# Softmax attention in a Macaron block: head pairs through DMA-built operands, or on 64 array rows each

## The chip, the cores and the metric

The kernel runs on one core of one Trainium2 chip. The metric is the device time of one launch in microseconds (us), lower is better. The engines are named as in the profile: PE is TensorE, DVE is VectorE, ACT is ScalarE, POOL is GpSimd, SP is SyncE, whose queue issues DMAs. PEld is the weight load of PE. PSUM is the memory that matmuls write, in banks of 128 x 512 f32.

## What is computed

The program is a chain of stages over x of 8 sequences x 512 tokens x 128 features: a feed-forward stage with block quantisation, softmax attention, the feed-forward stage again, a mixture of experts, six layers of linear attention, the mixture again. Only the softmax attention is touched:

```python
def _L0_attn_ref(x, Wq, Wk, Wv, Wo, bo):     # 16 heads of 64, x is (8, 512, 128)
    q, k, v = (split_heads(x @ W.T) for W in (Wq, Wk, Wv))
    sim = jnp.einsum('bhid,bhjd->bhij', q, k) * 64 ** -0.5
    m = jnp.max(sim, axis=-1, keepdims=True)
    e = jnp.exp(sim - m)
    attn = e / (jnp.sum(e, axis=-1, keepdims=True) + 1e-10)
    out = jnp.einsum('bhij,bhjd->bhid', attn, v)
    return merge_heads(out) @ Wo.T + bo
```

## The kernel before, in words

`attn_stage` works on 64 pairs of heads (8 sequences x 8 pairs), numbered g. It is a software pipeline: one turn of the loop over `PERIODS`, called a period here, does the scores of pair g+1, the exponentials of pair g, the values of pair g-1, the output product of pair g-2 and the projections of pair g+2. The order on each engine is written out by hand in that loop, and semaphores hold the engines together.

Of each pair:

- `project` (L840) makes q, k and v from f16 high and low parts of x and of the weights. `high` (ACT, L748) writes the f16 high part of q or k, `low` (DVE, L681) what is left of it as a second f16.
- `to_rows` (SP, L598) copies these by DMA, so that for each head the high part stands on array rows 0 to 63 and the low part, or the high part again, on rows 64 to 127. Ten DMAs a pair.
- `scores` (L807), eight units i of one head and one tile of 128 queries, is one 128-row matmul of 512 columns each into one of two PSUM banks; `neg_max` (DVE, L664) reads a unit's bank and writes the negated row maxima. After four units `max_turned` (L817) transposes them, `max_row` (DVE, L672) writes four rows of 128 in f16 and `max_row` (SP, L614) brings them by DMA to one row behind the low part.
- `scores_turned` (L824), eight units, is two 128-row matmuls into one of two other banks: all of high times high, high times low, low times high and minus the maximum. `exp` (ACT, L763) reads the bank.
- POOL (L648 to L656) adds up the exponentials of the four key tiles; `values` (PE, L862) sums them over the partitions with ones (L868) and multiplies with v (L875). Both use f32 and half of the array's columns for each head, and each f32 matmul is two instructions on the chip. `total_out` (ACT), `inv_total` (DVE, L689, a reciprocal over 128 x 512) and `normalise` (DVE, L693) follow, then `output` (PE, L879), which adds up in one bank over the eight pairs of a sequence, and `add_x` (DVE, L701).

Two kinds of waiting matter on PE. A unit of scores waits until DVE has read the bank that it overwrites (`s_read`), and `max_turned` until the last read of its head.

Of the kernel before, what the change touches and what calls it, by code (L numbers as in the profile page):

```python
# [543 lines left out]
def attn_stage(nc, mem, tag):  # L544

    with ExitStack() as ctx:
# [12 lines left out]
        nmax = [s.sb(f"nmax{i}", [P, P]) for i in range(2)]  # L561
        mrow = [s.sb(f"mrow{i}", [TPB, P], F16) for i in range(2)]
# [5 lines left out]
        (set_up, proj_done, hi_done, lo_done, v_out, s_done, s_read, t_done, exp_done, chain, added, sums_done, total_done,  # L568
         rinv_done, pv_done, o_done, out_done, biased, x_added) = (s.sem(n) for n in (
             "set_up", "proj_done", "hi_done", "lo_done", "v_out", "s_done", "s_read", "t_done", "exp_done", "chain",  # L570
             "added", "sums_done", "total_done", "rinv_done", "pv_done", "o_done", "out_done", "biased", "x_added"))
        s_in = [s.sem(f"s_in{i}") for i in range(RING)]
        t_in = [s.sem(f"t_in{i}") for i in range(RING)]
        m_in = [s.sem(f"m_in{i}") for i in range(2)]
        S_DMAS, T_DMAS = 8, 2
        halves = (slice(0, DH), slice(DH, P))
        live = lambda g: 0 <= g < PAIRS_ALL
        PERIODS = range(-2, PAIRS_ALL + 2)

        def bank_use(g, j):  # L580

            if g < 0:
                return j if j < 2 else j - 1
            if g == PAIRS_ALL - 1:
                return 9 + 10 * g
            return 9 + 10 * g + j

        UNIT_USE = (0, 1, 3, 4, 6, 7, 8, 9)
        TURN_USE = (5, 2)
        score_use = lambda g, i: bank_use(g - 1, UNIT_USE[i])  # L590
        turn_use = lambda g, head: bank_use(g - 1 + head, TURN_USE[head])

        with nc.Block() as block:

            @block.sync
            def _(sp):
                clear_spent(sp, mem)
                def to_rows(g, which, part_i):  # L598

                    src = part[which]  # L600
                    k = g % RING
                    for head in range(2):
                        rows = src[halves[head], part_i, :]
                        if which == 0 and part_i == 0:
                            sp.dma_start(both[k][0:DH, :, head, :], rows.unsqueeze(1).to_broadcast([DH, 2, SEQ])).then_inc(s_in[k], 16)
                        elif which == 0:
                            sp.dma_start(both[k][DH:P, 0, head, :], rows).then_inc(s_in[k], 16)
                        elif part_i == 0:
                            sp.dma_start(kh[k][0:DH, head, :], rows).then_inc(s_in[k], 16)
                            sp.dma_start(kh[k][DH:P, head, :], rows).then_inc(s_in[k], 16)  # L610
                        else:
                            sp.dma_start(kl[k][0:DH, head, :], rows).then_inc(t_in[k], 16)

                def max_row(g, head):  # L614

                    sp.wait_ge(s_read, turn_use(g, head) + 1)
                    sp.dma_start(both[g % RING][DH:DH + 1, 1, head, :].rearrange("o (t q) -> o t q", q=P), mrow[head][:])\
                      .then_inc(m_in[head], 16)

                sp.wait_ge(set_up, RING + 3)  # L620
                for g in PERIODS:
                    if live(g):
                        max_row(g, 1)
                    if live(g + 2):
                        if g + 2 >= RING:
                            sp.wait_ge(t_done, 8 * (g + 3 - RING))
                        sp.wait_ge(hi_done, 2 * (g + 2) + 1)
                        to_rows(g + 2, 0, 0)
                        sp.wait_ge(lo_done, 2 * (g + 2) + 1)
                        to_rows(g + 2, 0, 1)  # L630
                    if live(g + 1):
                        max_row(g + 1, 0)
                    if live(g + 2):
                        sp.wait_ge(hi_done, 2 * (g + 2) + 2)
                        to_rows(g + 2, 1, 0)
                        sp.wait_ge(lo_done, 2 * (g + 2) + 2)
                        to_rows(g + 2, 1, 1)

            @block.gpsimd
            def _(pool):  # L640
                links = 0
                for g in range(PAIRS_ALL):
                    for head in range(2):
                        if g >= 2:
                            pool.wait_ge(sums_done, g - 1)
# [17 lines left out]
            def _(dve):  # L663
# [54 lines left out]
                for g in PERIODS:  # L718
# [3 lines left out]
                    if live(g):  # L722
                        max_row(g, 1)
# [954 lines left out]
```

## Time and profile before

| | us |
|---|---|
| median of 3 runs | 2222.82 |
| lowest, highest | 2221.43, 2230.84 |
| the profiled execution | 2225.31 |
| its span, first to last instruction | 2223.6 |
| busy in the span: PE | 1599.6 |
| busy: DVE | 1569.2 |
| busy: POOL | 1028.3 |
| busy: ACT | 912.8 |

The rows further down are of two kinds. A row of the timeline begins with the start in us from the span's start and the duration; then come engine, line of the program, operation and what was written from what; "x3" means three instructions merged, and a bracket gives the idle time before and what ended it. The end of a matmul in a row is modelled: it lies some 0.17 us behind the time at which the next can start, so the pace of PE is read from one start to the next.

### The profile page before, as it was taken

To read this page: it belongs to the slowest core of one execution; us is meant where nothing else is said; L and a number is where in the kernel's file an instruction comes from. 1 tells how busy PE (TensorE), PEld (TensorE's weight loads), DVE (VectorE), ACT (ScalarE), POOL (GpSimd) and SP (SyncE) were. 2 spreads that over 40 slices of the span, in tenths; PEclk is the share of its full clock that TensorE was granted. 3 is DMA by queue.
4 is the path that set the end of the run, shared out by engine and by line. 5 is a ranking of instruction groups with operands and counts; after the bars stand their busy time and mean duration, and the time that the engine had idled before them with its cause. 6 is when DMAs were issued, how large, how long until landed. Compare 5 with 4: busy or idle time off the path is not lost. (4 is left out here: it accounts for less than half of the span.)

```text
span 2223.6 us, 29789 instructions
## 1 busy us (share of the span) xinstructions
PE 1599.6 (72%) x9139; PEld 934.4 (42%) x9139; DVE 1569.2 (71%) x3212; ACT 912.8 (41%) x2102; POOL 1028.3 (46%) x1332
## 2 busy tenths in 40 slices
PE   0546389999999999999965563158658888830686
PEld 0334134444444444444423343135437767730453
DVE  5887778878788888877878886336467777752563
ACT  0112255555555555555522221035336676610452
POOL 0111245555555555555532224635435555546353
PEclk9889599999999999999987895579879999955898
DMA  6000022222222222222200000122300000001224
GB/s 186 0 0 1 23 63 58 58 58 58 63 59 61 60 59 58 58 58 59 62 9 1 0 0 24 56 77 80 104 16 1 1 1 1 1 32 62 75 81 145
DMA packets 126010, 104.05 MB, mean 47 GB/s; under 512 B 19680, under 2 KB 120480, under 8 KB 125856
## 3 DMA queue, kind: packets, MB, share of 16 engines
q1 hardware_dynamic: 111616, 77.75, 13.6%
q0 software_dynamic: 8704, 18.89, 2.5%
q10 hardware_dynamic: 5536, 5.52, 0.8%
q8 instruction: 77, 1.26, 0.2%
q14 instruction: 77, 0.63, 0.1%
HBM read 29.32 MB, written 22.30 MB: 23 GB/s over the span
## 5 line engine op out<-in xcount | busy, mean ns | idle before, releaser
L770 ACT ACTIVATE at_pT<-at_turned 128x512 f32<-128x512 f32 x512 | 305.6, 597 | 290.3 <-PE at_turned L837 271.2
L669 DVE TENSOR_REDUCE at_nmax<-at_score 128x1 f32<-128x512 f32 x512 | 337.1, 680 | 69.8 <-PE at_score L814 66.8
L648 POOL TENSOR_TENSOR m_rows<-at_pT 128x512 f32<-128x512 f32 x128 | 162.5, 1269 | 375.1 <-ACT at_pT L770 375.1
L691 DVE RECIPROCAL m_rows<-m_rows 128x512 f32<-128x512 f32 x64 | 214.6, 3353 | 37.7 <-ACT m_rows L776 37.7
L875 PE MATMUL at_pv<-at_pT,at_v 128*64 128x512 f32 x1024 | 230.6, 592 | 0.0
L814 PE MATMUL at_score<-at_kh,at_both 128*128 128x512 f16 x512 | 196.7, 385 | 22.6 <-DVE at_nmax L669 17.0
L1056 POOL DMA_INDIRECT by_token<-m_ysb,m_dest x144 | 138.2, 960 | 144.7 <-DVE m_ysb L1136 109.5
L836 PE MATMUL at_turned<-at_both,at_kh 128*128 128x512 f16 x512 | 194.9, 381 | 0.4 <-ACT at_pT L770 0.3
L837 PE MATMUL at_turned<-at_both,at_kl 128*128 128x512 f16 x512 | 194.8, 380 | 0.0
L656 POOL TENSOR_TENSOR m_rows<-m_rows,at_pT 128x512 f32<-128x512 f32 x128 | 162.8, 1272 | 10.6 <-ACT at_pT L770 0.7
L652 POOL TENSOR_TENSOR m_rows<-m_rows,at_pT 128x512 f32<-128x512 f32 x128 | 162.7, 1271 | 10.4 <-ACT at_pT L770 0.5
L1050 POOL DMA_INDIRECT by_expert<-m_rows,m_slot x128 | 123.7, 966 | 90.7 <-DVE m_slot L1099 53.0
L419 PE MATMUL f_gate<-m_wguT,f_xqT 128*128 128x352 f32 x128 | 63.1, 581 | 104.2 <-DVEq L337 102.9
L1307 PE MATMUL m_h<-m_w,m_x 128*128 x432 | 113.8, 400 | 33.1 <-DVE m_x L1113 23.2
L875 PEld LDWEIGHTS at_pv<-at_pT,at_v 128*64 128x64 f32 x1024 | 73.6, 137 | 146.2 <-issue 146.2
L365 POOL TENSOR_TENSOR f_hq<-f_hg,f_hsc 128x704 f32<-128x704 f32 x32 | 44.4, 1386 | 194.3 <-DVEq L341 194.3
L854 PE MATMUL at_proj<-m_rows 128*128 128x512 f16 x384 | 107.1, 389 | 18.6 <-DVE at_kl L716 10.3
L115 DVE TENSOR_SCALAR la_xn<-la_y,la_ln_mean,la_ln_rstd 128x128 f32<-128x128 f32 x192 | 81.6, 486 | 52.4 <-POOLq L1478 52.4
L381 ACT ACTIVATE f_silu<-f_gate 128x704 f32<-128x704 f32 x32 | 24.2, 757 | 219.7 <-PE f_up L420 219.7
L814 PEld LDWEIGHTS at_score<-at_kh,at_both 128*128 128x128 f16 x512 | 49.5, 97 | 145.5 <-DVE at_nmax L669 61.7
L1296 PE MATMUL m_x<-m_ident,m_xin 128*128 128x128 f32 x144 | 23.0, 284 | 88.6 <-DMA m_xin<-by_expert 88.6
L1124 DVE SCALAR_TENSOR_TENSOR m_g<-m_h,m_xin,m_silu 128x256 f32<-128x256 f32 x144 | 65.3, 478 | 28.1 <-ACT m_silu L1220 14.3
(309 smaller groups left out, 3685.0 us busy)
## 6 DMA issues: line engine op xcount, KB each, us to landing
at_both<-at_part_q SPq DMA_DIRECT2D x128, 128.0 KB, 2.4
at_kh<-at_part_k SPq DMA_DIRECT2D x256, 64.0 KB, 2.0
m_xin<-by_expert SPq DMA_DIRECT2D x144, 72.0 KB
at_both<-at_part_q SPq DMA_DIRECT2D x128, 64.0 KB, 2.1
at_kl<-at_part_k SPq DMA_DIRECT2D x128, 64.0 KB
m_rows<-by_token SPq DMA_DIRECT2D x32, 256.0 KB, 4.8
by_token<-m_ysb,m_dest POOLq DMA_INDIRECT x144
m_x<-in_x SPq DMA_DIRECT2D x8, 256.0 KB, 4.7
```

The lines of the kernel that those rows point to most:

```text
L648: nc.gpsimd.tensor_tensor(acc, pT[g % 2][:, head, 0, :], pT[g % 2][:, head, 1, :], ALU.add).then_inc(chain, 1)
L652: nc.gpsimd.tensor_tensor(acc, acc, pT[g % 2][:, head, 2, :], ALU.add).then_inc(chain, 1)
L656: nc.gpsimd.tensor_tensor(acc, acc, pT[g % 2][:, head, 3, :], ALU.add).then_inc(added, 1)
L669: nc.vector.tensor_reduce(nmax[head][:, qt:qt + 1], score[use % 2][:], AX.X, ALU.max, negate=True)\
L691: nc.vector.reciprocal(rinv, total).then_inc(rinv_done, 1)
L770: nc.scalar.activation(pT[g % 2][:, head, kt, :], turned[i % 2][:], ACT.Exp).then_inc(exp_done, 1)
L814: nc.tensor.matmul(score[use % 2][:], both[k][:, 0, head, qt * P:(qt + 1) * P], kh[k][:, head, :], start=True, stop=True).then_inc(s_done, 1)
L836: nc.tensor.matmul(turned[i % 2][:], kh[k][:, head, tile], both[k][:, 0, head, :], start=True, stop=False)
L837: nc.tensor.matmul(turned[i % 2][:], kl[k][:, head, tile], both[k][:, 1, head, :], start=False, stop=True)\
L875: last = nc.tensor.matmul(pv[halves[head], :], vv[g % 4][:, kt, halves[head]], pT[g % 2][:, head, kt, :], start=(kt == 0), stop=(kt == TPB ...
L1050: nc.gpsimd.indirect_dma_start(dram_rows, bass.IndirectOffsetOnAxis(slot[:, k, t:t + 1], 0), rows[k][:, t, :], None).then_inc(scattered, 16)
L1056: nc.gpsimd.indirect_dma_start(mem["dram_y_all"], bass.IndirectOffsetOnAxis(dest[j // TPB % DESTS][:, j % TPB:j % TPB + 1], 0), ysb[q % YS ...
```

## The change

Each head of a pair now stays on the 64 array rows on which the projection puts it: head 0 on rows 0 to 63, head 1 on rows 64 to 127. The DMAs and their buffers are gone. The scores of a query tile are two 64-row matmuls, one for each head, of the high parts alone, into two banks, `score[0]` and `score[1]`. The turned scores of a key tile are three 64-row matmuls for each head, heads taking turns, then one of four rows for each head that subtracts the maxima: `mdiag` holds 4 x 512 for each head, four maxima rows laid out as a block diagonal, at rows 0 and 32. One transposition of `nmax` serves both heads, and one DVE operation, `max_rows`, multiplies it with the mask `own` into `mdiag`. The maxima are written over the scores' bank (`max_bank`), so the next pair's first scores wait for `m_out`. The program tells the array's shape for each matmul: 128 x 128, 128 rows x 64 columns for sums, values and the transposition, 64 rows x 128 columns for scores and turned scores, 32 x 128 for the maxima.

The order moves as well. On DVE the reciprocal (now `invert`) comes between the reads of query tiles 1 and 2, and `normalise` a period later. On PE the sums and the first values come after the scores of tile 1, the other values are spread over tiles 2 and 3, and v of pair g is projected at the end of period g. POOL alternates the heads. There is one period more at the end.

PE before, the start of a period, from the transposition of head 1's maxima (`at_score<-m_ident,at_nmax`) to the projection of q:

```order
L822 MATMUL at_score<-m_ident,at_nmax 128x128 [waits at_s_read]
L814 MATMUL at_score<-at_kh,at_both 128x512 [waits at_s_read]
L836 MATMUL at_turned<-at_both,at_kh 128x512 [waits at_exp_done]
L837 MATMUL at_turned<-at_both,at_kl 128x512
L854 MATMUL at_proj<-m_rows 128x512 [waits at_v_out]
L854 MATMUL at_proj<-m_rows 128x512 x2
```

PE now, the same engine in the stretch from the third key tile's turned scores to the end of a period:

```order
L755 MATMUL at_turned<-at_high_q,at_high_k 128x512 [waits at_exp_done] x2
L755 MATMUL at_turned<-at_low_q,at_high_k 128x512 x2
L755 MATMUL at_turned<-at_high_q,at_low_k 128x512 x2
L760 MATMUL at_turned<-at_mdiag,at_unit 128x512 x2
L738 MATMUL at_score<-at_high_k,at_high_q 128x512 [waits at_s_read]
L738 MATMUL at_score<-at_high_k,at_high_q 128x512
L804 MATMUL at_pv<-at_pT,at_v 64x512 x2
L743 MATMUL at_score<-m_ident,at_nmax 64x128 [waits at_s_read]
L804 MATMUL at_pv<-at_pT,at_v 64x512 x2
L786 MATMUL at_proj<-m_rows 128x128 [waits at_v_out,at_lo_done]
L786 MATMUL at_proj<-m_rows 128x128 x11
```

Where one unit was three matmuls of 128 rows, a tile is now ten of 64 or four rows, and the transposition stands between two blocks of values.

DVE before, one period, from a pair's reciprocal to the next pair's:

```order
L691 RECIPROCAL m_rows<-m_rows 128x512 [waits at_total_done]
L669 TENSOR_REDUCE at_nmax<-at_score 128x1 [waits at_s_done] x2
L699 TENSOR_TENSOR at_oT<-at_pv,m_rows 128x512 [waits at_out_done,at_rinv_done,at_pv_done]
L669 TENSOR_REDUCE at_nmax<-at_score 128x1 [waits at_s_done] x4
L678 TENSOR_SCALAR at_mrow<-at_score 4x128 [waits at_m_in1,at_s_done]
L669 TENSOR_REDUCE at_nmax<-at_score 128x1 [waits at_s_done] x2
L686 SCALAR_TENSOR_TENSOR at_part_q<-at_proj,at_part_q 128x512 [waits at_hi_done]
L678 TENSOR_SCALAR at_mrow<-at_score 4x128 [waits at_m_in0,at_s_done]
L686 SCALAR_TENSOR_TENSOR at_part_k<-at_proj,at_part_k 128x512 [waits at_hi_done]
```

DVE now, one period in the same way:

```order
L635 RECIPROCAL m_rows<-m_rows 128x512 [waits at_o_done,at_total_done]
L612 TENSOR_REDUCE at_nmax<-at_score 128x1 [waits at_s_done] x2
L628 SCALAR_TENSOR_TENSOR at_low_k<-at_proj,at_high_k 128x512 [waits at_t_done,at_hi_done]
L612 TENSOR_REDUCE at_nmax<-at_score 128x1 [waits at_s_done] x2
L620 TENSOR_TENSOR at_mdiag<-at_score,at_own 64x512 [waits at_t_done,at_m_done]
L612 TENSOR_REDUCE at_nmax<-at_score 128x1 [waits at_s_done,at_m_done]
L612 TENSOR_REDUCE at_nmax<-at_score 128x1 [waits at_s_done]
L642 TENSOR_TENSOR at_oT<-at_pv,m_rows 128x512 [waits at_out_done,at_rinv_done,at_pv_done]
L628 SCALAR_TENSOR_TENSOR at_low_q<-at_proj,at_high_q 128x512 [waits at_t_done,at_hi_done]
L612 TENSOR_REDUCE at_nmax<-at_score 128x1 [waits at_s_done] x2
```

Behind the reciprocal there are now four reads, the low part of k and the maxima before the pair's scores are done; before it was six reads and the normalisation.

The core of the diff; the functions that it takes away are printed above and left out here, and so are ACT's order and the semaphores' names:

```diff
-        both = [s.sb(f"both{i}", [P, 2, 2, SEQ], F16) for i in range(RING)]
-        kh = [s.sb(f"kh{i}", [P, 2, SEQ], F16) for i in range(RING)]
-        kl = [s.sb(f"kl{i}", [P, 2, SEQ], F16) for i in range(RING)]
-        part = [s.sb(f"part_{n}", [P, 2, SEQ], F16) for n in "qk"]
-        vv = [s.sb(f"v{i}", [P, TPB, P]) for i in range(4)]
+        QUAD = P // 4
+        high_of = [[s.sb(f"high_{n}{i}", [P, SEQ], F16) for i in range(RING)] for n in "qk"]
+        low_of = [[s.sb(f"low_{n}{i}", [P, SEQ], F16) for i in range(RING)] for n in "qk"]
+        vv = [s.sb(f"v{i}", [P, TPB, P]) for i in range(2)]
         pT = [s.sb(f"pT{i}", [P, 2, TPB, SEQ]) for i in range(2)]
...
-        nmax = [s.sb(f"nmax{i}", [P, P]) for i in range(2)]
-        mrow = [s.sb(f"mrow{i}", [TPB, P], F16) for i in range(2)]
+        nmax = s.sb("nmax", [P, 2 * QUAD])
+        own = s.sb("own", [2 * QUAD, TPB])
+        mdiag = s.sb("mdiag", [2 * QUAD, TPB, P], F16)
+        unit = s.sb("unit", [2 * QUAD, P], F16)
...
         score = [s.bank(f"score{i}") for i in range(2)]
...
+        max_bank = score[0][0:2 * QUAD, 0:P]
...
                 for g in range(PAIRS_ALL):
...
+                    if g >= 2:
+                        pool.wait_ge(sums_done, g - 1)
+                    for kt in range(1, TPB):
+                        for head in range(2):
+                            acc = psum[g % 2][:, head, :]
+                            before = pT[g % 2][:, head, 0, :] if kt == 1 else acc
+                            pool.wait_ge(exp_done, 8 * g + 2 * kt + head + 1)
+                            if kt > 1:
+                                pool.wait_ge(chain, 4 * g + 2 * (kt - 2) + head + 1)
+                            done = nc.gpsimd.tensor_tensor(acc, before, pT[g % 2][:, head, kt, :], ALU.add)
+                            done.then_inc(chain if kt < TPB - 1 else added, 1)
...
+                def neg_max(g, qt):
+                    if qt == 0 and g:
+                        dve.wait_ge(m_done, g)
+                    for head in range(2):
+                        dve.wait_ge(s_done, 8 * g + 2 * qt + head + 1)
+                        nc.vector.tensor_reduce(nmax[:, head * QUAD + qt:head * QUAD + qt + 1], score[head][:], AX.X, ALU.max, negate=True)\
+                          .then_inc(s_read, 1)
+
+                def max_rows(g):
+                    dve.wait_ge(m_done, g + 1)
                     if g:
...
+                        dve.wait_ge(t_done, 8 * g)
+                    wide = [2 * QUAD, TPB, P]
+                    nc.vector.tensor_tensor(mdiag[:], max_bank.unsqueeze(1).to_broadcast(wide), own[:].unsqueeze(2).to_broadcast(wide),
+                                            ALU.mult).then_inc(m_out, 1)
 
                 def low(g, which):
...
                     dve.wait_ge(hi_done, 2 * g + 1 + which)
+                    if g >= RING:
+                        dve.wait_ge(t_done, 8 * (g - RING + 1))
                     scale = (DH ** -0.5 / W_ATTN, 1.0 / W_ATTN)[which]
...
+                    nc.vector.scalar_tensor_tensor(out=low_of[which][g % RING][:], in0=proj[:], scalar=scale,
+                                                   in1=high_of[which][g % RING][:], op0=ALU.mult, op1=ALU.subtract).then_inc(lo_done, 1)
+
+                def invert(g):
                     dve.wait_ge(total_done, g + 1)
+                    if g:
+                        dve.wait_ge(o_done, g)
                     nc.vector.reciprocal(rinv, total).then_inc(rinv_done, 1)
...
                 for g in PERIODS:
                     if live(g + 1):
                         neg_max(g + 1, 0)
+                    if live(g - 2):
+                        normalise(g - 2)
+                    if live(g + 2):
+                        low(g + 2, 0)
+                    if live(g - 3) and (g - 3) % PAIRS == PAIRS - 1:
+                        add_x((g - 3) // PAIRS)
+                    if live(g + 1):
                         neg_max(g + 1, 1)
-                    if live(g):
-                        max_row(g, 1)
+                    if live(g - 1):
+                        invert(g - 1)
                     if live(g + 1):
                         neg_max(g + 1, 2)
-                        neg_max(g + 1, 3)
-                    if live(g + 2):
-                        low(g + 2, 0)
-                    if live(g + 1):
-                        max_row(g + 1, 0)
                     if live(g + 2):
                         low(g + 2, 1)
-                    if live(g - 1):
-                        inv_total(g - 1)
                     if live(g + 1):
-                        neg_max(g + 1, 4)
-                        neg_max(g + 1, 5)
-                    if live(g - 1):
-                        normalise(g - 1)
-                    if live(g + 1):
-                        neg_max(g + 1, 6)
-                        neg_max(g + 1, 7)
-                    if live(g - 2) and (g - 2) % PAIRS == PAIRS - 1:
-                        add_x((g - 2) // PAIRS)
+                        neg_max(g + 1, 3)
+                        max_rows(g + 1)
...
+                def scores(g, qt):
+                    if qt == 0:
+                        pe.wait_ge(hi_done, 2 * g + 2)
+                    if g or qt:
+                        pe.wait_ge(s_read, 8 * g + 2 * qt)
+                    if g and qt == 0:
+                        pe.wait_ge(m_out, g)
+                    for head in range(2):
+                        rows = halves[head]
+                        nc.tensor.matmul(score[head][:], high_of[0][g % RING][rows, qt * P:(qt + 1) * P], high_of[1][g % RING][rows, :],
+                                         start=True, stop=True).then_inc(s_done, 1)
+
+                def max_turned(g):
+                    pe.wait_ge(s_read, 8 * (g + 1))
+                    nc.tensor.transpose(max_bank, nmax[:], mem["ident"][:]).then_inc(m_done, 1)
+
+                def scores_turned(g, kt):
                     k = g % RING
                     tile = slice(kt * P, (kt + 1) * P)
...
                     if kt == 0:
...
+                        pe.wait_ge(lo_done, 2 * g + 2)
+                    for n, (k_of, q_of) in enumerate(((high_of, high_of), (high_of, low_of), (low_of, high_of))):
+                        for head in range(2):
+                            if n == 0 and (g or kt):
+                                pe.wait_ge(exp_done, 8 * g + 2 * kt + head - 1)
+                            rows = halves[head]
+                            nc.tensor.matmul(turned[head][:], k_of[1][k][rows, tile], q_of[0][k][rows, :], start=(n == 0), stop=False)
+                    if kt == 0:
+                        pe.wait_ge(m_out, g + 1)
+                    for head in range(2):
+                        rows = slice(head * QUAD, head * QUAD + TPB)
+                        nc.tensor.matmul(turned[head][:], unit[rows, :], mdiag[rows, :, :].rearrange("p t q -> p (t q)"), start=False,
+                                         stop=True).then_inc(t_done, 1)
 
...
+                def add_up(g):
                     pe.wait_ge(added, 2 * (g + 1))
                     if g:
                         pe.wait_ge(total_done, g)
                     for head in range(2):
                         last = nc.tensor.matmul(sums[halves[head], :], ones[:], psum[g % 2][:, head, :], start=True, stop=True)
                     last.then_inc(sums_done, 1)
...
+
+                def values(g, kt):
+                    if kt == 0:
+                        pe.wait_ge(v_out, g + 1)
+                        if g:
+                            pe.wait_ge(o_done, g)
+                    for head in range(2):
+                        last = nc.tensor.matmul(pv[halves[head], :], vv[g % 2][:, kt, halves[head]], pT[g % 2][:, head, kt, :],
+                                                start=(kt == 0), stop=(kt == TPB - 1))
+                    if kt == TPB - 1:
+                        last.then_inc(pv_done, 1)
...
-                    for i in range(UPP):
+                    for kt in range(TPB):
+                        if live(g):
+                            scores_turned(g, kt)
                         if live(g + 1):
-                            scores(g + 1, i)
-                        if live(g):
-                            scores_turned(g, i)
-                        if i == 1 and live(g):
-                            max_turned(g, 1)
-                        if i == 2 and live(g + 2):
-                            project(g + 2, 0)
-                        if i == 3:
-                            if live(g - 2):
-                                output(g - 2)
+                            scores(g + 1, kt)
+                        if kt == 0:
+                            if live(g + 2):
+                                project(g + 2, 0)
+                            if live(g - 3):
+                                output(g - 3)
+                        elif kt == 1 and live(g - 1):
+                            add_up(g - 1)
+                            values(g - 1, 0)
+                        elif kt == 2:
                             if live(g + 2):
                                 project(g + 2, 1)
+                            if live(g - 1):
+                                values(g - 1, 1)
+                        elif kt == 3:
+                            if live(g - 1):
+                                values(g - 1, 2)
                             if live(g + 1):
-                                max_turned(g + 1, 0)
+                                max_turned(g + 1)
                             if live(g - 1):
-                                values(g - 1)
-                        if i == 6 and live(g + 2):
-                            project(g + 2, 2)
+                                values(g - 1, 3)
+                            if live(g):
+                                project(g, 2)
```

## Rows read from the trace of the kernel before

**Rows 1.** Busy time of each engine by stretch, the pipeline's steady part.

```profile
core 0: us, PE busy (x) PEld busy (x) DVE busy (x) ACT busy (x) POOL busy (x), PEclk, DMA share, GB/s
290.00:1120.00 830.00, 806.39 (x4409) 358.69 (x4409) 666.30 (x868) 440.39 (x738) 474.91 (x377) 1.00 0.24 60
```

**Rows 2.** Timeline, PE and its weight loads (PEld), one period from 701 us.

```profile
701.13 0.38 PE L836 MATMUL at_turned<-at_both,at_kh 128*128 128x512 f16 x1
701.13 0.10 PEld L837 LDWEIGHTS at_turned<-at_both,at_kl 128*128 128x128 f16 x1
...
701.56 0.81 PE L854 MATMUL at_proj<-m_rows 128*128 128x512 f16 x3
...
702.21 0.38 PE L814 MATMUL at_score<-at_kh,at_both 128*128 128x512 f16 x1
...
702.86 1.05 PE L887 MATMUL at_out<-m_woT,at_oT 128*128 128x128 f32 x8
...
703.97 0.82 PE L854 MATMUL at_proj<-m_rows 128*128 128x512 f16 x3
...
704.63 0.27 PE L822 MATMUL at_score<-m_ident,at_nmax 128*128 128x128 f32 x1
...
704.83 0.20 PEld L868 LDWEIGHTS at_sums<-m_rows 128*64 128x64 f32 x4 [0.28 <-issue]
704.83 1.08 PE L868 MATMUL at_sums<-m_rows 128*64 128x512 f32 x4
...
705.74 3.60 PE L875 MATMUL at_pv<-at_pT,at_v 128*64 128x512 f32 x16
...
709.28 0.39 PE L814 MATMUL at_score<-at_kh,at_both 128*128 128x512 f16 x1
...
711.23 0.83 PE L858 MATMUL at_proj<-m_rows 128*128 128x128 f16 x12
...
711.90 0.38 PE L814 MATMUL at_score<-at_kh,at_both 128*128 128x512 f16 x1
...
713.85 0.27 PE L822 MATMUL at_score<-m_ident,at_nmax 128*128 128x128 f32 x1
...
715.02 0.81 PE L854 MATMUL at_proj<-m_rows 128*128 128x512 f16 x3
```

**Rows 3.** Timeline, ACT and DVE, the same period.

```profile
702.41 0.60 ACT L755 ACTIVATE at_part_q<-at_proj 128x512 f16<-128x512 f32 x1
...
702.63 0.69 DVE L669 TENSOR_REDUCE at_nmax<-at_score 128x1 f32<-128x512 f32 x1 [0.60 <-PE at_score L814]
...
703.24 0.68 DVE L686 SCALAR_TENSOR_TENSOR at_part_q<-at_proj,at_part_q 128x512 f16<-128x512 f32 x1
...
705.96 0.60 ACT L776 ACTIVATE m_rows<-at_sums 128x512 f32<-128x512 f32 x1 [0.53 <-PE at_sums L868]
...
706.59 3.35 DVE L691 RECIPROCAL m_rows<-m_rows 128x512 f32<-128x512 f32 x1 [0.44 <-ACT m_rows L776]
...
709.86 1.22 DVE L669 TENSOR_REDUCE at_nmax<-at_score 128x1 f32<-128x512 f32 x2
...
711.00 0.68 DVE L699 TENSOR_TENSOR at_oT<-at_pv,m_rows 128x512 f32<-128x512 f32 x1
...
711.59 2.71 DVE L669 TENSOR_REDUCE at_nmax<-at_score 128x1 f32<-128x512 f32 x4
...
714.22 0.27 DVE L678 TENSOR_SCALAR at_mrow<-at_score 4x128 f16<-4x128 f32 x1
```

**Rows 4.** Waits, 252 to 1150 us, PE for a DMA: us in total, times, longest.

```profile
PE at_score L814 <- DMA at_kh<-at_part_k: 5.5, 3, 2.5
```

**Rows 5.** Timeline, start of the attention stage.

```profile
252.65 0.17 DVE L708 MEMSET at_nmax<- 128x128 f32 x1 [3.93 <-PEq L483]
...
260.14 1.46 PE L854 MATMUL at_proj<-m_rows 128*128 128x512 f16 x3 [10.25 <-DVE at_kl L716]
```

More of the change, by code:

```diff
@@ L597, in _ @@
                 clear_spent(sp, mem)
[L598 to L612, printed above, removed]
@@ L681, in low @@
                 def low(g, which):
                     dve.wait_ge(hi_done, 2 * g + 1 + which)
+                    if g >= RING:
+                        dve.wait_ge(t_done, 8 * (g - RING + 1))
                     scale = (DH ** -0.5 / W_ATTN, 1.0 / W_ATTN)[which]
-                    pair = part[which]
-                    nc.vector.scalar_tensor_tensor(out=pair[:, 1, :], in0=proj[:], scalar=scale, in1=pair[:, 0, :], op0=ALU.mult,
-                                                   op1=ALU.subtract).then_inc(lo_done, 1)
@@ L785, in _ @@
                     if live(g):
[L786 to L788 removed]
+                        exp(g, 1)
                     if live(g - 1):
@@ L801, in _ @@
                 XY = [(0, 0), (0, 1), (1, 0)]
-                def bank_free(use):
-                    if use >= 2:
-                        pe.wait_ge(s_read, use - 1)
-                def scores(g, i):
-                    head, qt = divmod(i, TPB)
-                    use = score_use(g, i)
-                    k = g % RING
-                    if i == 0:
-                        pe.wait_ge(s_in[k], 16 * S_DMAS * (g // RING + 1))
-                    bank_free(use)
-                    nc.tensor.matmul(score[use % 2][:], both[k][:, 0, head, qt * P:(qt + 1) * P], kh[k][:, head, :], start=True,
-                                     stop=True).then_inc(s_done, 1)
@@ L833, in scores_turned @@
-                    n = 8 * g + i
-                    if n >= 2:
-                        pe.wait_ge(exp_done, n - 1)
-                    nc.tensor.matmul(turned[i % 2][:], kh[k][:, head, tile], both[k][:, 0, head, :], start=True, stop=False)
-                    nc.tensor.matmul(turned[i % 2][:], kl[k][:, head, tile], both[k][:, 1, head, :], start=False, stop=True)\
-                      .then_inc(t_done, 1)
+                        pe.wait_ge(lo_done, 2 * g + 2)
[5 more added lines that the diff above has]
+                            nc.tensor.matmul(turned[head][:], k_of[1][k][rows, tile], q_of[0][k][rows, :], start=(n == 0), stop=False)
@@ L869, in values @@
                     last.then_inc(sums_done, 1)
-                    pe.wait_ge(v_out, g + 1)
-                    if g:
-                        pe.wait_ge(o_done, g)
-                    for kt in range(TPB):
-                        for head in range(2):
-                            last = nc.tensor.matmul(pv[halves[head], :], vv[g % 4][:, kt, halves[head]], pT[g % 2][:, head, kt, :],
-                                                    start=(kt == 0), stop=(kt == TPB - 1))
-                    last.then_inc(pv_done, 1)
+                def values(g, kt):
+                    if kt == 0:
+                        pe.wait_ge(v_out, g + 1)
+                        if g:
+                            pe.wait_ge(o_done, g)
+                    for head in range(2):
+                        last = nc.tensor.matmul(pv[halves[head], :], vv[g % 2][:, kt, halves[head]], pT[g % 2][:, head, kt, :],
+                                                start=(kt == 0), stop=(kt == TPB - 1))
+                    if kt == TPB - 1:
+                        last.then_inc(pv_done, 1)
                 def output(g):
```

160 lines of the change are left out of this document (41 added, 119 removed).

## The prediction

> **What bounds the kernel now.** I read first the busy time by stretch: from 290 to 1120 us PE is busy 806 of 830 us at full clock, DVE 666, POOL 475, ACT 440, and the DMA engines 0.24 of their time [rows 1]. So PE is the bound of the attention stage, and DVE is next. Then the timeline of one period. The projection of q begins at 701.56 and the next one at 715.02 [rows 2]: a period is 13.46 us, and the 830 us hold 62 of them. PE's row durations overlap, so I price by starts [rows 2]. Two f16 matmuls of 512 columns take 701.13 to 701.56, 0.215 each, and three take 0.65 (701.56 to 702.21). Twelve of 128 columns take 0.67 (711.23 to 711.90). Eight f32 instructions of 128 columns last 1.05 with a last one of about 0.27, so 0.11 each and 0.89 in all. Sums and values, twenty f32 instructions of half the columns, take 704.83 to 709.28, 4.45.
>
> The values' sixteen took 3.54 (705.74 to 709.28). One f32 instruction of 512 columns is two f16 slots, 0.43. One after the other sixteen would be 6.9; in pairs they are 3.44. So matmuls on two halves of the columns do run at once here, and about 0.10 is left over at the end, where the array goes back to the full shape. At the entry it is alike: the transposition starts at 704.63, is worth 0.11, and the sums start at 704.83 together with their weight load, which elsewhere comes a matmul ahead (the load of 701.13 runs beside the matmul of 701.13) [rows 2]. I call this a shape change and price it at 0.10.
>
> PE's period before: 24 score slots 5.16, projections 1.30 and 0.67, sums and values 4.35, output 0.89, two transpositions 0.22, two shape changes 0.20: 12.79. The other 0.67 of 13.46 is waiting.
>
> **What the change does to PE.** A tile's scores become two 64-row matmuls, its turned scores six, its maxima two of four rows. If the two heads run at once, as column halves do, that is 1 + 3 + 1 slots a tile, 20 a period or 4.30: 0.86 less. One transposition goes, 0.11 less. The sum is 11.62 without shape changes. But now the shape changes often. Between the 64-row, 32-row, full and half-column shapes I count 18 in a period: four in tile 0, with the one from the period before, four in tile 1, five in tile 2, five in tile 3. At 0.10 they cost 1.80, and PE's work is 13.42, just the old period. No row shows a change between row shapes. From below it could cost nothing, from above I take twice the column price, 0.20. I take 0.10, the one price that rows show.
>
> The Trainium skill (TensorEngine Tiling (Array Packing), Key Properties) says that changing the tiling mode, not just the tile, drains TensorE. The rows show such a stall for columns only; by the page all 18 would pay, which is the value taken.
>
> **What the change does to DVE.** The work is about the same: eight reads, two low parts, reciprocal, normalisation, and one `max_rows` of 512 elements, at most the 0.68 of the normalisation [rows 3], for two of 0.27. Its place is what counts. With data at hand DVE starts a read 0.57 after the one before (two from 709.86 to 711.00), the normalisation's successor 0.59 after it (711.00 to 711.59), and the read behind the reciprocal 3.27 after its start (706.59 to 709.86) [rows 3]. PE goes on 0.73 after the start of the DVE operation that it waits for (703.24 [rows 3] to 703.97 [rows 2]).
>
> Before, the reciprocal lay beside the values' 3.54 on PE, in which no scores were wanted. Now PE does 0.86 of values and then wants scores of tile 2 and 3, whose reads stand behind the reciprocal. This closes a loop from one reciprocal to the next:
>
> - DVE: reciprocal 3.27, two reads 1.14, low part of k 0.59, first read of tile 3 0.57, and from the start of the last read to the transposition on PE 0.73: 6.30.
> - PE, transposition to sums: 0.11, last values 0.86, v 0.67, turned scores and maxima of tile 0 0.86, scores 0.215, q 0.65, output 0.89, turned scores and maxima of tile 1 0.86, scores 0.215: 5.33, and nine shape changes.
> - Sums to reciprocal: 1.13 to `total_out` (704.83 to 705.96) and 0.63 more (706.59) [rows 2, 3].
>
> That is 13.4 with free shape changes and 14.3 with nine at 0.10. PE has 13.42 of work in it, so 0.9 is waiting, which must stand before the scores of tile 3 (they wait for reads behind the reciprocal) and before the transposition (it waits for both reads of tile 3, with only 0.86 of values to do meanwhile). In both the longest single wait is under 1 us, so I leave the clock at full.
>
> **The rest.** The ten DMAs a pair, SP's queue and their buffers go: PE waited for them three times in the whole stage, 5.5 us [rows 4], so in the steady part that is worth nothing. ACT and POOL have the same operations in another order; both had half of the period free [rows 1], and that room hides it. `max_rows` ends about 1.1 after the transposition (713.85 [rows 2] to 714.22 [rows 3], then 0.73), while PE still has 0.86 + 0.67 + 0.65 to do before the maxima are wanted: hidden, with 1 us to spare. At the start 7.5 us of memsets (252.65 to 260.14) shrink to some 2 [rows 5], and the 5.5 of waits for DMAs go: 11 us gained once. The end stays a chain of the same steps: nothing.
>
> **The sum.** 62 x (14.30 - 13.46) = 52, less 11, is 41 us more on the profiled execution's 2225.3 (its span is 2223.6). That execution lies 2.5 above the median of the runs, 2222.8, so I forecast 2264 us.
>
> **The rivals.**
>
> - **A, the forecast**: heads run at once, a shape change costs 0.07 to 0.13. 14.0 to 14.6 a period: 2245 to 2283. Chance 0.50.
> - **B, not slower**: changes between row shapes are free, and only those to and from the half-column shape pay. It is one mechanism, in the loop above: two of its nine changes are of that kind, so the period is 13.6, 9 us more over 62, less 11: 2221. If those are free too, 13.4 gives 2208. It decides below 0.02 a change. For it: column halves take other columns of results, row halves only feed other rows, and no row shows that this needs a stop. Against it: at 704.83 even the weight load waited [rows 2]. Chance 0.20.
> - **C, dearer**: a change costs 0.2, or the loads of the next 64 rows are not hidden (20 slots with a load of 0.10 [rows 2] exposed in each is 2.0 a period, the same size). PE's work is 15.2 then, 15.6 with 0.4 of waiting before the transposition: 62 x 2.14 - 11 = 122, 2345. Chance 0.15.
> - **D, the change doesn't do what it says**: the heads' matmuls don't run at once, 20 slots more, 4.30. PE's work is 17.7: 62 x 4.24 - 11 = 252, 2475; with free shape changes 15.9 and 2363. For it: no row shows two row halves at once. Against: the column halves do it. Chance 0.12.
>
> In this trace the weight load for the next matmul on the same rows runs beside the present one (both at 701.13 [rows 2]). The Trainium skill (TensorE: Matmul & The Clock Gate, What overlaps and what doesn't) says that a load overlaps matmuls in flight only when the row group differs; by that rule each head's next matmul would wait for its load, which is C's second form, and the row speaks against it. The same page gives 3.07 for four row tiles instead of 4; an estimate by that ratio makes the 20 slots 5.6 instead of 4.3, some 80 us more, between A and C. No row here shows it.
>
> **How the numbers follow.** 0.03 is left for what I don't see. About 0.5% is what a measurement of this kernel tells from no change, so the bounds are 2211.7 and 2233.9. Faster: nearly half of B, 0.09. Same: the rest of B and the cheap end of A, 0.16. Slower: 0.75. The range goes from just under B's lower end, 2207, over A and C to the cheap end of D, 2385; most of D is left out.
>
> **What would show it.** In the trace after: two rows of the turned scores that start together, or 0.2 apart (D). The start of the first maxima matmul 0.10 later than 0.65 after the first turned one (A), or not (B). The third scores pair some 0.3 late and the transposition some 0.6 late, both released by `neg_max`, and ACT and POOL idle beside it. A period of 14.3 from one q projection to the next. If PE never waits for `neg_max`, my loop is wrong; if the clock falls below 1.00, all prices are too low.

## The result

| | before | changed |
|---|---|---|
| median, us | 2224.31 | 2276.23 |
| lowest, highest | 2221.43, 2230.84 | 2271.47, 2277.21 |
| span of the profiled execution | 2223.6 | 2275.1 |

The changed kernel is slower: 1.0225 times the time of before, 95% interval 1.0197 to 1.0253. The forecast was 2264, and slower. The DMAs of the attention stage are gone, and so is any wait for them; PE is busy for longer, 1660.7 us of the span against 1599.6.

This is PE's timeline of the changed kernel over the end of one period and all of the next, with one row of its weight loads and with DVE's and ACT's rows that stand in the loop of the prediction. "x2" are the two heads' matmuls.

```profile
700.99 0.82 PE L781 MATMUL at_proj<-m_rows 128*128 128x512 f16 x3
...
701.64 1.05 PE L816 MATMUL at_out<-m_woT,at_oT 128*128 128x128 f32 x8
...
702.63 0.39 PE L755 MATMUL at_turned<-at_high_q,at_high_k 64*128 64x512 f16 x2
702.64 0.10 PEld L755 LDWEIGHTS at_turned<-at_low_q,at_high_k 64*128 64x128 f16 x2
702.86 0.38 PE L755 MATMUL at_turned<-at_low_q,at_high_k 64*128 64x512 f16 x2
...
703.07 0.38 PE L755 MATMUL at_turned<-at_high_q,at_low_k 64*128 64x512 f16 x2
703.38 0.39 PE L760 MATMUL at_turned<-at_mdiag,at_unit 4*128 4x512 f16 x2
703.70 0.39 PE L738 MATMUL at_score<-at_high_k,at_high_q 64*128 64x512 f16 x2
...
704.02 1.08 PE L795 MATMUL at_sums<-m_rows 128*64 128x512 f32 x4
...
705.15 0.60 ACT L706 ACTIVATE m_rows<-at_sums 128x512 f32<-128x512 f32 x1 [0.26 <-PE at_sums L795]
705.78 3.35 DVE L635 RECIPROCAL m_rows<-m_rows 128x512 f32<-128x512 f32 x1 [0.36 <-ACT m_rows L706]
...
709.05 1.22 DVE L612 TENSOR_REDUCE at_nmax<-at_score 128x1 f32<-128x512 f32 x2
...
709.81 0.39 PE L760 MATMUL at_turned<-at_mdiag,at_unit 4*128 4x512 f16 x2
710.19 0.68 DVE L628 SCALAR_TENSOR_TENSOR at_low_k<-at_proj,at_high_k 128x512 f16<-128x512 f32 x1
...
710.33 0.39 PE L738 MATMUL at_score<-at_high_k,at_high_q 64*128 64x512 f16 x2
710.65 1.08 PE L804 MATMUL at_pv<-at_pT,at_v 128*64 128x512 f32 x4
710.78 1.28 DVE L612 TENSOR_REDUCE at_nmax<-at_score 128x1 f32<-128x512 f32 x2
...
712.12 0.30 PE L743 MATMUL at_score<-m_ident,at_nmax 128*64 128x128 f32 x1 [0.40 <-DVE at_nmax L612]
712.35 1.08 PE L804 MATMUL at_pv<-at_pT,at_v 128*64 128x512 f32 x4
...
713.36 0.84 PE L786 MATMUL at_proj<-m_rows 128*128 128x128 f16 x12
714.14 0.39 PE L755 MATMUL at_turned<-at_high_q,at_high_k 64*128 64x512 f16 x2
...
715.21 0.39 PE L738 MATMUL at_score<-at_high_k,at_high_q 64*128 64x512 f16 x2
...
715.53 0.82 PE L781 MATMUL at_proj<-m_rows 128*128 128x512 f16 x3
```

From one q projection to the next is 14.54 us (700.99 to 715.53), against 13.46 before [rows 2]. Three pairs of 64-row matmuls start 0.22 apart (702.63, 702.86, 703.07), so both heads fit in one slot: they run at once. To the four-row pair it is 0.31, and from there to the scores 0.32 (703.38 to 703.70), each a slot of 0.215 and 0.10 for the change of shape. The scores of tile 3 come 0.52 after the maxima of their tile (709.81 to 710.33) where others come 0.32 after: 0.20 of waiting for the reads behind the reciprocal. The transposition comes 1.47 after the values that it follows (710.65 to 712.12), which take 1.01 elsewhere (712.35 to 713.36): 0.46 of waiting.

The stage's start and end, from the first write of its setup to the first turned scores, and its last operation; of the changed kernel:

```profile
251.18 0.11 DVE L650 MEMSET at_nmax<- 128x64 f32 x1 [3.91 <-PEq L483]
...
252.08 1.46 PE L781 MATMUL at_proj<-m_rows 128*128 128x512 f16 x3 [3.64 <-DVE at_own L656]
...
266.94 0.61 PE L755 MATMUL at_turned<-at_high_q,at_high_k 64*128 64x512 f16 x2
```

```profile
1198.43 0.69 DVE L648 TENSOR_TENSOR m_x<-at_out,m_x 128x512 f32<-128x512 f32 x1 [1.25 <-PE at_out L816]
```

and the same last operation of the kernel before:

```profile
1150.64 0.69 DVE L706 TENSOR_TENSOR m_x<-at_out,m_x 128x512 f32<-128x512 f32 x1 [1.25 <-PE at_out L887]
```

The stage took 947.9 us (251.18 to 1199.12) and before 898.7 (252.65 [rows 5] to 1151.33). That is 49.2 of the 51.5 between the spans; the other 2.3 come up in stages that the change doesn't touch (1.5 less ahead of this one, 3.7 more behind it). The 64 reciprocals give the mean period and the start apart. Their first and last starts, of the kernel before and of the changed one:

```profile
L691 DVE RECIPROCAL m_rows<-m_rows x64: 3352/3353/3354, 301.4 to 1145.3; 128x512 f32<-128x512 f32 x64
```

```profile
L635 DVE RECIPROCAL m_rows<-m_rows x64: 3352/3353/3353, 284.6 to 1193.0; 128x512 f32<-128x512 f32 x64
```

Over 63 periods 843.9 became 908.4: 13.40 to 14.42 us each, 64.5 in all. From the stage's start to the first reciprocal 48.8 became 33.4, 15.4 less. Part of that is the clock. In the kernel before, PE waited 2.48 for a DMA, and after it worked at the lower of its two clock levels, 1.2 GHz, until 286 us: the granted clock is 0.51 from 280 to 286, where a slot takes 0.43. In the changed kernel the granted clock is 1.00 from 271 us to the first reciprocal. The wait and the stretch of the kernel before, and the stretch of the changed one (columns as in [rows 1], the granted clock is the third number from the end):

```profile
280.53 0.61 PE L814 MATMUL at_score<-at_kh,at_both 128*128 128x512 f16 x1 [2.48 <-DMA at_kh<-at_part_k]
```

```profile
280.00:286.00 6.00, 5.47 (x14) 2.14 (x15) 2.35 (x4) 1.79 (x3) 1.72 (x2) 0.51 0.10 24
```

```profile
271.00:285.00 14.00, 12.15 (x81) 4.08 (x79) 9.56 (x15) 8.31 (x15) 9.04 (x8) 1.00 0.01 1
```

### The profile page after: what moved, and what is told of

The parts are those of the page before. It is cut to its first block and busy times, and to the rows that moved or that the text cites. A ratio compares the mean times of both kernels' runs of the same rounds, so it can differ in the third digit from the quotient of the medians.

```text
span 2275.1 us, 30856 instructions
## 1 busy us (share of the span) xinstructions
PE 1660.7 (73%) x10099; PEld 874.6 (38%) x10099; DVE 1561.2 (69%) x3141; ACT 880.7 (39%) x2102; POOL 1022.4 (45%) x1332
## 5 line engine op out<-in xcount | busy, mean ns | idle before, releaser
L612 DVE TENSOR_REDUCE at_nmax<-at_score 128x1 f32<-128x512 f32 x512 | 324.9, 676 | 188.2 <-PE at_score L738 188.1
L700 ACT ACTIVATE at_pT<-at_turned 128x512 f32<-128x512 f32 x512 | 277.9, 594 | 301.1 <-PE at_turned L760 301.1
L804 PE MATMUL at_pv<-at_pT,at_v 128*64 128x512 f32 x1024 | 272.0, 611 | 0.0
L692 ACT ACTIVATE at_v<-at_proj 128x512 f32<-128x512 f32 x64 | 38.2, 597 | 185.2 <-PE at_proj L786 185.2
L738 PE MATMUL at_score<-at_high_k,at_high_q 64*128 64x512 f16 x512 | 100.8, 390 | 11.7 <-DVE at_nmax L612 3.0
L755 PE MATMUL at_turned<-at_high_q,at_high_k 64*128 64x512 f16 x512 | 101.5, 388 | 0.5 <-ACT at_pT L700 0.4
L760 PE MATMUL at_turned<-at_mdiag,at_unit 4*128 4x512 f16 x512 | 99.4, 385 | 0.0
L755 PE MATMUL at_turned<-at_low_q,at_high_k 64*128 64x512 f16 x512 | 98.6, 377 | 0.0
L755 PE MATMUL at_turned<-at_high_q,at_low_k 64*128 64x512 f16 x512 | 98.5, 377 | 0.0
L804 PEld LDWEIGHTS at_pv<-at_pT,at_v 128*64 128x64 f32 x1024 | 56.7, 135 | 86.9 <-issue 79.4
```

The lines of the kernel that those rows point to most:

```text
L612: nc.vector.tensor_reduce(nmax[:, head * QUAD + qt:head * QUAD + qt + 1], score[head][:], AX.X, ALU.max, negate=True)\
L700: nc.scalar.activation(pT[g % 2][:, head, kt, :], turned[head][:], ACT.Exp).then_inc(exp_done, 1)
L738: nc.tensor.matmul(score[head][:], high_of[0][g % RING][rows, qt * P:(qt + 1) * P], high_of[1][g % RING][rows, :], start=True, stop=True). ...
L755: nc.tensor.matmul(turned[head][:], k_of[1][k][rows, tile], q_of[0][k][rows, :], start=(n == 0), stop=False)
L760: nc.tensor.matmul(turned[head][:], unit[rows, :], mdiag[rows, :, :].rearrange("p t q -> p (t q)"), start=False, stop=True).then_inc(t_don ...
L804: last = nc.tensor.matmul(pv[halves[head], :], vv[g % 2][:, kt, halves[head]], pT[g % 2][:, head, kt, :], start=(kt == 0), stop=(kt == TPB ...
```

## The experiments

**Theory L**: the period is the loop from one reciprocal to the next, over DVE's reads and PE's queue, with 0.10 for each change of shape. **Rival W**: the period is PE's own work, and the reciprocal's place costs nothing. Periods below run from one start of v's projection to the next, medians between 300 and 1080 us, where they repeat to 0.01; read so, the changed kernel's is 14.54, and that is the one to compare with. (The mean between the first and the last reciprocal would not do: it also moves when the reciprocal is moved.) Times are beside runs of before on the same chip (median 2227.79 for the first four).

**Maxima in the scores' shape** (`e1_max64`).

```diff
-        nmax = s.sb("nmax", [P, 2 * QUAD])
-        own = s.sb("own", [2 * QUAD, TPB])
-        mdiag = s.sb("mdiag", [2 * QUAD, TPB, P], F16)
-        unit = s.sb("unit", [2 * QUAD, P], F16)
+        nmax = s.sb("nmax", [P, P])
+        own = s.sb("own", [P, TPB])
+        mdiag = s.sb("mdiag", [P, TPB, P], F16)
+        unit = s.sb("unit", [P, P], F16)
...
-                        rows = slice(head * QUAD, head * QUAD + TPB)
+                        rows = halves[head]
```

> The changed kernel with the maxima's block diagonal spread over each head's 64 rows (zeros in rows 4 to 63), so that its matmuls have the shape of the scores; the transposition becomes a full 128 x 128. Shape changes on PE fall from 18 to 12 a period, on the loop through the reciprocal from 9 to 6, and the transposition costs 0.11 in place of 0.23. Theory L (the period is the loop from one reciprocal to the next, at 0.10 a shape change): period 14.5 less 0.42, 14.1 us, time 2276 - 26 = 2250. Rival W (the period is PE's own work, the reciprocal's place costs nothing): 0.72 less, 13.8, time 2231. If shape changes were free: 2270 or more.

Measured 2251.59, ratio 1.0106 (1.0077 to 1.0134), period 14.15 for L's 14.1. One tile of its timeline, PE, with the slot of the maxima now like the others:

```profile
707.41 0.39 PE L755 MATMUL at_turned<-at_high_q,at_high_k 64*128 64x512 f16 x2
707.64 0.38 PE L755 MATMUL at_turned<-at_low_q,at_high_k 64*128 64x512 f16 x2
707.85 0.38 PE L755 MATMUL at_turned<-at_high_q,at_low_k 64*128 64x512 f16 x2
708.07 0.38 PE L760 MATMUL at_turned<-at_mdiag,at_unit 64*128 64x512 f16 x2
708.28 0.38 PE L738 MATMUL at_score<-at_high_k,at_high_q 64*128 64x512 f16 x2
...
714.07 0.38 PE L760 MATMUL at_turned<-at_mdiag,at_unit 64*128 64x512 f16 x2
714.90 0.39 PE L738 MATMUL at_score<-at_high_k,at_high_q 64*128 64x512 f16 x2 [0.45 <-DVE at_nmax L612]
```

The maxima follow 0.22 after and the scores 0.21 after them, so the 0.10 goes with the shape, not with the operation. But the scores of tile 3 now wait longer (0.83 from 714.07 to 714.90): PE reaches them sooner and DVE doesn't. Of the 0.72 of work that the expectation counts, 0.39 came out. That is L, not W.

**The reciprocal at the end of the period** (`e2_inv_end`).

```diff
                         neg_max(g + 1, 1)
-                    if live(g - 1):
-                        invert(g - 1)
...
                         max_rows(g + 1)
+                    if live(g - 1):
+                        invert(g - 1)
```

> The changed kernel with one thing moved: the reciprocal stands on DVE behind the pair's maxima, at the end of the period, in place of between the reads of tiles 1 and 2. Theory L: the loop is opened, the scores of tile 3 wait no longer, PE's work with its 18 shape changes and the wait of some 0.4 before the transposition are left: period 14.2, time 2276 - 19 = 2257. Rival W: no change, 2276. If the reads of tile 0 behind the reciprocal now come too late: slower than 2276.

Measured 2260.11, ratio 1.0141 (1.0122 to 1.0160), period 14.32 (708.15 to 722.47 below) for L's 14.2, 0.22 less than the changed kernel's. W's 2276 is excluded: against 1.0225 the interval lies clear. In the steady part PE's matmuls wait for DVE at the transposition alone:

```profile
PE at_score L743 <- DVE at_nmax L612: 21.1, 57, 0.4
```

```profile
708.15 0.84 PE L786 MATMUL at_proj<-m_rows 128*128 128x128 f16 x12
...
722.47 0.84 PE L786 MATMUL at_proj<-m_rows 128*128 128x128 f16 x12
```

**Both** (`e3_both`).

> Both edits, maxima in 64 rows and the reciprocal at the end of the period. Theory L: with the loop opened the six saved shape changes count in full, period 13.4, time 2276 - 70 = 2206, below the kernel before. Rival W: as the first edit alone, 2231. The sum of the two single gains would be 2231 as well by L, so anything near 2206 says that the loop and the shape changes hid one another.

Measured 2214.38, ratio 0.9926 (0.9904 to 0.9949), period 13.51. The single gains are 0.39 and 0.22 us a period, both together 1.03: each edit alone runs into what the other takes away. With the reciprocal at the end the 64-row maxima are worth 0.81, alone 0.39. The time is 8 us above L's figure and 17 below W's; put to the 2224.31 that these figures started from, the ratio gives 2208, 2 above L's. What PE still waits for is the transposition:

```profile
706.55 1.08 PE L804 MATMUL at_pv<-at_pT,at_v 128*64 128x512 f32 x4
...
708.00 0.33 PE L743 MATMUL at_score<-m_ident,at_nmax 128*128 128x128 f32 x1 [0.37 <-DVE at_nmax L612]
...
709.27 0.84 PE L786 MATMUL at_proj<-m_rows 128*128 128x128 f16 x12
```

**The reciprocal in halves, the transposition behind the values** (`e4_split`), with the maxima in 64 rows.

```diff
-                    nc.vector.reciprocal(rinv, total).then_inc(rinv_done, 1)
+                    nc.vector.reciprocal(rinv[:, 0:SEQ // 2], total[:, 0:SEQ // 2])
+
+                def invert_rest(g):
+                    nc.vector.reciprocal(rinv[:, SEQ // 2:], total[:, SEQ // 2:]).then_inc(rinv_done, 1)
...
                         max_rows(g + 1)
+                    if live(g - 1):
+                        invert_rest(g - 1)
...
-                            if live(g + 1):
-                                max_turned(g + 1)
                             if live(g - 1):
                                 values(g - 1, 3)
+                            if live(g + 1):
+                                max_turned(g + 1)
```

> Maxima in 64 rows; the reciprocal in two halves of 256 columns, one in its place of the changed kernel, one at the end of the period; the transposition behind the last values, so that they cover the reads of tile 3. Theory L: no read of scores is late for longer than PE has other work, shape changes 10 a period, period 12.8, time 2276 - 107 = 2169. Rival W: 12.8 of work too if the halves cost nothing, but then the first edit alone would have shown 13.8 or less. If each half costs much more than 1.68 on DVE: 2190 or more.

Measured 2167.20, ratio 0.9726 (0.9706 to 0.9745), period 12.81 for L's 12.8. This version beats both kernels. DVE's timeline shows the two halves, each between reads that are not late:

```profile
701.76 1.74 DVE L638 RECIPROCAL m_rows<-m_rows 128x256 f32<-128x256 f32 x1
703.42 1.22 DVE L612 TENSOR_REDUCE at_nmax<-at_score 128x1 f32<-128x512 f32 x2
...
707.54 1.74 DVE L635 RECIPROCAL m_rows<-m_rows 128x256 f32<-128x256 f32 x1
709.20 1.22 DVE L612 TENSOR_REDUCE at_nmax<-at_score 128x1 f32<-128x512 f32 x2
```

PE's rows around the transposition:

```profile
711.73 1.94 PE L809 MATMUL at_pv<-at_pT,at_v 128*64 128x512 f32 x8
713.60 0.33 PE L748 MATMUL at_score<-m_ident,at_nmax 128*128 128x128 f32 x1
713.76 0.83 PE L791 MATMUL at_proj<-m_rows 128*128 128x128 f16 x12
```

From the start of the last two blocks of values to v's projection it is 2.03 (711.73 to 713.76), and in `e3_both`, with the transposition between the blocks, 2.72 (706.55 to 709.27). These 0.69 are nearly all of the 0.70 between the two periods, so the gain over `e3_both` lies at the transposition, which no longer waits. No run moves the transposition and leaves the reciprocal whole, so what the halves add by themselves is not shown.

**The reciprocal cut short in its place** (`e7_short`).

```diff
-                    nc.vector.reciprocal(rinv, total).then_inc(rinv_done, 1)
+                    nc.vector.reciprocal(rinv[:, 0:64], total[:, 0:64]).then_inc(rinv_done, 1)
```

> The changed kernel with seven eighths of the inversion left out: from the third pair on the reciprocal covers 64 of 512 columns, some 0.5 us in place of 3.35; the rest of rinv keeps old values, so the output is not the reference's. Its place stays. Theory L: the loop through the reciprocal falls below PE's own work, which with the wait before the transposition is 14.2: time 2276 - 19 = 2257, as when the reciprocal was moved, not 3 us a period less. Rival W (PE's own work alone): 2276. Rival DVE (the reciprocal counts in full): 14.5 - 2.8, time 2100.

Measured 2267.11 beside 2232.28 for before, ratio 1.0161 (1.0131 to 1.0192); 1.0161 of 2224.31 is 2260, for L's 2257. Against the expectation's words the edit leaves out seven eighths of every reciprocal, not from the third pair on only:

```profile
L635 DVE RECIPROCAL m_rows<-m_rows x64: 552/553/554, 284.3 to 1178.2; 128x64 f32<-128x64 f32 x64
```

The period is 14.32, 0.22 less for 2.8 us less of DVE work, and the same to 0.01 as in `e2_inv_end`. So the loop through the reciprocal held the period up by what it stood above PE's work with its wait before the transposition, and no more; moving the reciprocal did as much as leaving most of it out. The rival in which it counts in full, 2100, is out.

**Shape changes alone** (`e8_split_max32`): the version in halves with `nmax`, `own`, `mdiag`, `unit` and the maxima's rows as in the changed kernel.

> The fastest version so far (reciprocal in two halves, transposition behind the last values, maxima in 64 rows, 2167) with the maxima in 4 rows of a 32-row shape again, as in the changed kernel. There PE never waited for the reads, so this prices shape changes without a loop in between: 18 a period against 10, and the transposition to half the columns 0.23 against 0.11. At 0.10 a change: 0.92 a period, 2167 + 57 = 2224. If the saved time of the 64-row maxima came from elsewhere (from the loop alone): 2167 to 2180.

Measured 2224.19 beside 2232.28 for before, ratio 0.9964 (0.9952 to 0.9976), period 13.63. Against 12.81 that is 0.81 for eight changes of shape, 0.10 each. In the steady part of neither does the profile show a wait of PE for a read. That the time met 2224 is partly luck: 0.9964 of the 2227.79 beside the first version is 2220. The other 0.12 of the expected 0.92 was for the transposition, and it didn't come. PE's rows around it:

```profile
711.72 1.94 PE L809 MATMUL at_pv<-at_pT,at_v 128*64 128x512 f32 x8
713.59 0.30 PE L748 MATMUL at_score<-m_ident,at_nmax 128*64 128x128 f32 x1
713.73 0.83 PE L791 MATMUL at_proj<-m_rows 128*128 128x128 f16 x12
```

To v's projection it is 2.01 (711.72 to 713.73), where the version in halves, with its transposition in the full shape, takes 2.03. The transposition starts 1.87 after the values in both (713.59, 713.60). Eight value instructions are worth 1.72 and a block behind another shape 0.05 more (the four sums took 0.91 before, 704.83 to 705.74 [rows 2]), so 0.10 is left before the transposition even here, where the shape stays 128 x 64. It is as if the transposition to half the columns stood in a shape of its own; why, no run tells.

**Head by head** (`e5b_by_head`).

```diff
-                    for n, (k_of, q_of) in enumerate(((high_of, high_of), (high_of, low_of), (low_of, high_of))):
-                        for head in range(2):
+                    for head in range(2):
+                        for n, (k_of, q_of) in enumerate(((high_of, high_of), (high_of, low_of), (low_of, high_of))):
```

> The changed kernel with the six 64-row matmuls of a tile's turned scores issued head by head, three for head 0 and then three for head 1, in place of heads taking turns. Same work, same number of shape changes. If two row halves run at once only where neighbours in the queue lie on different halves (theory L's reading of the rows that start together), the six take 5 slots of 0.215 in place of 3: 1.7 us more work on PE a period, and with the rest of the loops some 1.5 more, time 2276 + 93 = 2369. Rival: PE starts what is further back in its queue by itself, then nothing changes, 2276.

Measured 2201.72 beside 2152.01 for before on that chip, ratio 1.0228 (1.0207 to 1.0250): the changed kernel's 1.0225; the period is 14.56, for 14.54. My expectation fell. PE's timeline:

```profile
691.83 0.40 PE L755 MATMUL at_turned<-at_high_q,at_high_k 64*128 64x512 f16 x2
692.05 0.39 PE L755 MATMUL at_turned<-at_low_q,at_high_k 64*128 64x512 f16 x2
692.27 0.39 PE L755 MATMUL at_turned<-at_high_q,at_low_k 64*128 64x512 f16 x2
```

Head 1's first matmul stands three places behind head 0's in the program, and still they start together. The single records, unmerged, hold a trace of the order: the two starts of such a pair lie 0.010 us apart in 748 of the 750 pairs recorded, and in the changed kernel 0.003 or 0.004 in 748 of 750. That speaks against an order that was changed back on the way to the chip, and for PE starting work of a free half ahead of instructions that still wait for the other. No run shows this directly.

## Why the prediction was right, and by how much it was off

- **The heads run at once**: right, by the rows that start together. D is out.
- **A shape change costs 0.10, between row shapes as between column shapes**: right. 0.31 and 0.32 in the timeline of the changed kernel, 0.22 where the shape stays, and 0.81 for eight by two runs. B and C are out. The drain that the Trainium skill describes (TensorEngine Tiling (Array Packing), Key Properties) shows for row shapes too. The rule of the Trainium skill that a load overlaps matmuls only on other rows (TensorE: Matmul & The Clock Gate, What overlaps and what doesn't) doesn't show: the load for each head's next matmul started at 702.64, beside its present one on the same rows (702.63), and the next followed 0.22 after, one slot, with no 0.10 for a load between them.
- **The loop through the reciprocal**: right in mechanism. DVE's part was 6.34 (705.78 to 712.12) for 6.30, sums to reciprocal 1.76 (704.02 to 705.78) for 1.76. PE's part with nine changes was 6.44 (712.12 to 715.53, then from the q projection at 700.99 to 704.02) for 6.23. The term that was mis-sized is the transposition: 0.23 to the next start, not 0.11, though the values behind it have its shape, so the count of nine lacks one; and 0.05 more for a block of values that stands alone. Some 0.04 stay open. The period was 14.54 for 14.30, and the granted clock was 1.00 from 290 to 1120 us, as I had left it.
- **The waits**: 0.20 before the scores of tile 3 and 0.46 before the transposition, for 0.3 and 0.6. With more work on PE in the same loop there was less to wait for.
- **The start**: 15.4 us gained, not 11. Setup fell from 7.5 to 0.9 (I left it 2), and the 5.5 of waits for DMAs went. That is 12.1. I had not counted the clock: 5.3 us of PE's work before (280.53 to 285.84) ran at half speed behind a wait for a DMA, an estimate of 2.7 that the changed kernel saves. Nor had I counted that v's projection no longer stands ahead of the first scores; its share isn't measured.
- **The sum**: 64.5 in place of 52 for the periods, 15.4 in place of 11 for the start, 2.3 from the other stages: 51.5 in the profiled executions, for 41. The two misses have opposite signs, so the total is nearer than its terms.

## What to carry to other kernels

Count the changes of the array's shape in a period before splitting a matmul into smaller tiles: here each cost 0.10 us, and padding four rows with zeros to the neighbours' 64 took eight of them away and added nothing to their slots (0.22). Where two engines take turns in a loop, look for the longest operation of the engine that isn't the bound, and ask what is queued behind it: put where the other engine has work of its own, whole at the end of the period or in halves, the same reciprocal made PE wait for no read of scores. And put an operation that must wait behind work that doesn't: the transposition behind the last values was worth 0.69 us a period. Gains of two edits on such a loop don't add up one by one; try them together.

## What the runs showed of the hardware that I had not expected

Matmuls on the two row halves ran in pairs also where the program issues three for one half and then three for the other (starts 691.83, 692.05, 692.27; period 14.56 for 14.54). An f32 transposition that starts as soon as its wait ends kept PE for 0.23 to half the columns (712.12 to 712.35); with no wait ahead of it, between the values and v's projection, 0.14, and 0.10 more before it, although the values have its shape.
